# Router logits as plain fp32 matmuls in column groups, with a new order of VectorE's work around the router

## The chip, the cores and the metric

The kernel runs on one NeuronCore of a Trainium2 chip. The metric is the device time of one execution, in microseconds. Each time shown is from the device; the table below gives the median of three runs and, beside it, the one execution that the hardware profiler recorded, from which all rows come.

## What is computed

The input x has 4096 tokens (16 sequences of 256) of 128 channels. It is layer-normed to xn, and two branches work on xn:

```python
# mixer: a linear recurrence over time in each channel
r, alpha, g = sigmoid(lin(x_r, W_r)), sigmoid(lin(x_a, W_a)), sigmoid(lin(x_g, W_g))
k, v, decay = tanh(lin(x_k, W_k)), lin(x_v, W_v), exp(-softplus(lin(x_w, W_w)))
state = state * decay + alpha * k * v          # scan over 256 steps
s = (groupnorm(r * state) * gn_w + gn_b) * g @ W_out.T + b_out
# experts: four rounds, each adds to the current value
for r in range(4):
    logits = cur @ Wg[r] + bg[r]               # 4 experts
    cw = softmax over the two largest, 0 for the others
    hmid = gelu(cur @ W1[e] + b1[e])           # 128 -> 512, every expert
    cur = cur + sum over e of cw[e] * (hmid @ W2[e] + b2[e])
out = x + s * silu(cur)
```

where lin(mix, W) is (xn + (previous xn - xn) * mix) @ W.T. All experts are computed for all tokens; the gates only weigh them.

## The kernel before, in words

**Data and tiles.** Channels lie on the 128 partitions, tokens along the free dimension. `cur` [128, 4096] holds the current value in eight blocks of 512 tokens. Matmuls are in the one-pass type float32r (f32r); to get fp32 products, an operand is split into a high part (f32r) and a low part (the rest), and three matmuls are added: high weight by high data, low weight by high data, high weight by low data (`mm_high` and `mm_low`, L848 to L853).

**Steps.** The expert work is a list of 128 steps (STEPS = 4 rounds x 8 blocks x 4 experts). Step s is turn k = s // 4 (a round and a block) and expert e = s % 4. TensorE's loop (L959) does in step s: `up(s + 1)`, 12 matmuls of 512 columns into four PSUM banks; `down(s)`, 12 matmuls (eight with g_hi, L909 and L910, then four with g_lo, L914) into one of two y banks; then what the tables put there. ScalarE's `hidden(s + 1)` (L374) takes the four banks through gelu in two halves and copies each half to g_hi (L386). VectorE's step s (L766) makes g_lo of step s + 1 in two halves (`g_low_half`, L614, instruction L619), and `combine(s)` (L622, instruction L633) multiplies the y bank by the gates into `tmp`, which POOL's DMA adds to `cur` (L322). down(s) waits for g_hi and g_lo by halves and for combine(s - 2), since there are two y banks (`combined`, L904; it starts at 2 through L757, so down(2) waits for combine(0)).

**Router.** For each turn the logits of four experts are needed. Turns are taken in batches (BATCHES, L36): two of two turns, then seven of four. LOGITS_AT (L53) gives the step of TensorE at which a batch is done: 0, 6, 12, 28, 44, 60, 76, 92 and 108. `logits(n)` (L918) uses f32r operands: `wg_hl` holds Wg's high and low parts side by side (8 columns a round), `wg_pad` is a strip of zeros with these 8 columns in the middle, and a window of 128 columns on it puts the result of turn i on PSUM rows 32 i. Every turn adds its two matmuls (cur_lo, L926; cur_hi, L927) into the same full bank `rb`. `router_scores(n)` (L570) on VectorE transposes the bank, adds high and low columns (L581), adds bg (L582), ranks the four logits and leaves the argument of a tanh; ScalarE's `router_tanh` (L369) takes it; `router_gates(n)` (L602) makes `cw`. SyncE's `spread_gates(k)` (L247) writes cw to DRAM and reads it back on all partitions as `cw_b`, for turn 0 with the first expert's share first (L262). For n of 3 and more VectorE does the scores one step after the logits, behind both halves of g_lo, and the gates two steps after the logits.

**Splitting.** `split_cur(k)` (L545) makes cur_hi and cur_lo of a turn (five buffers); it also copies the round's Wg columns to `wg_pad` (L563).

**Mixer.** Sixteen sequences m, each with stages 0 to 7 at steps 15 + 7 m + stage (`mixers_at`, L58). On VectorE: stages 0 to 2 `mixer_input` (L644; xm_hi L659, xm_lo L661), stage 3 `mixer_scan` (L664; st L673), stage 4 `mixer_norm` (L676, mn L689), stage 6 `mixer_gate`. On TensorE they are projected or transposed at the end of the same step (the norm's result one step later).

**End.** From step 101 on a block b is finished every four steps. `end_scaled(b)` (L705) and `end_product(b)` (L716) stand at the start of VectorE's step 102 + 4 b, TensorE's `turn_product(b)` (L866) transposes the product between up() and down() of step 103 + 4 b, `end_output(b)` (L724) adds x at VectorE's step 103 + 4 b, and SyncE stores it. The last block is done behind the loop.

**Order.** Every engine's order is written out by hand; VectorE's is lines 733 to 844. LATE (L55) holds steps 0 and 8: their combine stands one step later, ahead of the next combine, since their gates come late.

## Time and profile before

| | us |
|---|---|
| median of three runs | 824.88 |
| lowest, highest | 821.72, 825.96 |
| the profiled execution | 823.14 |
| its span, first to last instruction | 821.3 |
| mean granted TensorE clock | 0.993 of full |

How to read the rows below. PE is TensorE's matmul, PEld its weight load, DVE VectorE, ACT ScalarE, POOL GpSimd, SP SyncE. A row of a timeline is: start in us from the span's start, length in us, engine, line of the kernel, operation, output and input by the program's names, shape, count. Brackets hold the idle time before the instruction and what released it. Matmuls overlap in their pipeline and their ends are modelled, so the cost of a matmul is read from start to start, not from its length; a count over 1 merges neighbours of the same line. The granted clock is a share of full speed: 1.00 is the 2.4 GHz level, 0.50 the 1.2 GHz level.

### The profile page before, as it was taken

Reading aid. Unit: us, or ns where it says so; the run is one execution under the profiler, and the core shown is the slowest. Engines: PE = TensorE matmul, PEld = TensorE weight load, DVE = VectorE, ACT = ScalarE, POOL = GpSimd, SP = SyncE. Lnnn points to the kernel's source line nnn. Section 1 sums busy time; section 2 is a strip of 40 time slices with the busy share of each in tenths; the row PEclk is TensorE's granted clock in tenths of the full one; section 3 lists DMA queues with packets and bytes.
Section 4 is the critical chain, followed back from the end, with each engine's and each line's share of the span. In section 5 each row is a group of like instructions: output and inputs, shape, how many; then the busy total and the mean of one; then the engine's idle time right before and its main releaser. Section 6 shows DMA issues by size and latency. Waiting matters only on the chain. (4 is left out here: it accounts for less than half of the span.)

```text
span 821.3 us, 10635 instructions
## 1 busy us (share of the span) xinstructions
PE 803.9 (98%) x3656; PEld 651.3 (79%) x3656; DVE 714.8 (87%) x1339; ACT 652.2 (79%) x911; POOL 115.0 (14%) x135
## 2 busy tenths in 40 slices
PE   8899999999999999999999999999999999899996
PEld 7787788888788887888888887888878888678885
DVE  6978888889997979988898898898989898889897
ACT  7798887887887877888788886888778887678874
POOL 0010211111111111111111101111111111011110
PEclk9999999999999999999999999999999999999998
DMA  9333463342533415423164422644226343174532
GB/s 255 116 78 91 102 162 84 96 97 39 143 59 83 97 33 142 103 49 94 29 152 100 95 39 39 142 103 104 39 54 164 93 116 72 19 180 115 129 65 51
DMA packets 44468, 78.50 MB, mean 96 GB/s; under 512 B 6656, under 2 KB 23552, under 8 KB 40448
## 3 DMA queue, kind: packets, MB, share of 16 engines
q0 software_dynamic: 18144, 33.04, 23.9%
q1 hardware_dynamic: 25136, 44.64, 16.5%
q8 instruction: 29, 0.48, 0.2%
q10 hardware_dynamic: 1136, 0.16, 0.1%
q14 instruction: 23, 0.19, 0.1%
HBM read 40.34 MB, written 2.36 MB: 52 GB/s over the span
## 5 line engine op out<-in xcount | busy, mean ns | idle before, releaser
L382 ACT ACTIVATE g<-h_bank,b_c 128x512 f32<-128x512 f32 x512 | 329.3, 681 | 80.2 <-PE h_bank L853 78.5
L619 DVE TENSOR_TENSOR g_lo<-g,g_hi 128x1024 fp32r<-128x1024 f32 x256 | 307.9, 1221 | 73.6 <-ACT g_hi L386 72.6
L386 ACT ACTIVATE g_hi<-g 128x1024 fp32r<-128x1024 f32 x256 | 271.7, 1062 | 8.1
L322 POOL DMA_DIRECT2D cur<-tmp x126 | 113.9, 904 | 692.1 <-DVE tmp L633 572.4
L849 PE MATMUL h_bank<-cur_hi,w_hi 128*128 128x512 f32 x512 | 206.3, 403 | 1.2 <-ACT g L382 0.7
L909 PE MATMUL y_bank<-g_hi,w_hi 128*128 128x512 f32 x512 | 203.4, 397 | 2.8 <-issue 2.2
L853 PE MATMUL h_bank<-cur_lo,w_hi 128*128 128x512 f32 x512 | 204.1, 399 | 0.0
L850 PE MATMUL h_bank<-cur_hi,w_lo 128*128 128x512 f32 x512 | 203.1, 397 | 0.0
L910 PE MATMUL y_bank<-g_hi,w_lo 128*128 128x512 f32 x512 | 203.0, 397 | 0.0
L914 PE MATMUL y_bank<-g_lo,w_hi 128*128 128x512 f32 x512 | 140.9, 396 | 2.2 <-DVE g_lo L619 2.2
L909 PEld LDWEIGHTS y_bank<-g_hi,w_hi 128*128 128x128 f32 x512 | 96.5, 188 | 26.5 <-issue 2.6
L914 PEld LDWEIGHTS y_bank<-g_lo,w_hi 128*128 128x128 f32 x512 | 96.3, 188 | 26.2 <-DVE g_lo L619 3.1
L853 PEld LDWEIGHTS h_bank<-cur_lo,w_hi 128*128 128x128 f32 x512 | 96.6, 189 | 23.7 <-DVE cur_lo L567 0.4
L910 PEld LDWEIGHTS y_bank<-g_hi,w_lo 128*128 128x128 f32 x512 | 96.6, 189 | 23.4
L849 PEld LDWEIGHTS h_bank<-cur_hi,w_hi 128*128 128x128 f32 x512 | 97.0, 189 | 20.5 <-ACT g L382 1.1
L850 PEld LDWEIGHTS h_bank<-cur_hi,w_lo 128*128 128x128 f32 x512 | 96.7, 189 | 19.2
L633 DVE SCALAR_TENSOR_TENSOR tmp<-y_bank,b_c,cw_b 128x512 f32<-128x512 f32 x128 | 94.9, 743 | 1.4 <-DMA cur<-tmp 1.3
L653 DVE SCALAR_TENSOR_TENSOR xm<-xx,mix,xn_t 128x256 f32<-128x256 f32 x96 | 42.0, 479 | 0.6
L661 DVE TENSOR_TENSOR xm_lo<-xm,xm_hi 128x512 fp32r<-128x512 f32 x48 | 33.2, 693 | 1.6
L853 PE MATMUL p_bank<-xm_lo,pj_hi 128*128 128x256 f32 x96 | 27.6, 288 | 0.9 <-DVE xm_lo L661 0.9
L849 PE MATMUL p_bank<-xm_hi,pj_hi 128*128 128x256 f32 x96 | 27.5, 286 | 0.8 <-DVE xm_hi L659 0.8
L850 PE MATMUL p_bank<-xm_hi,pj_lo 128*128 128x256 f32 x96 | 27.0, 281 | 0.0
(120 smaller groups left out, 516.9 us busy)
## 6 DMA issues: line engine op xcount, KB each, us to landing
cur<-tmp POOLq DMA_DIRECT2D x126, 256.0 KB, 3.4
cw_b<-cw_scratch SPq DMA_DIRECT2D x31, 1024.0 KB, 5.1
cur<-in_x SPq DMA_DIRECT2D x8, 256.0 KB, 5.5
xn_t<-cur SPq DMA_DIRECT2D x8, 256.0 KB, 2.8
xr<-in_x SPq DMA_DIRECT2D x8, 256.0 KB, 3.2
out<-o SPq DMA_DIRECT2D x7, 256.0 KB, 2.4
cw_b<-in_w SPq DMA_DIRECT2D x4, 256.0 KB, 5.2
cw_b<-cw_scratch SPq DMA_DIRECT2D x1, 768.0 KB, 5.2
```

The source lines that it names most:

```text
L322: pool.dma_start(cur[:, block_of(s // E)], tmp[:, s % 2, :], accum_op=ALU.add).then_inc(summed, DMA)
L382: nc.scalar.activation(g[:, gb, ft * BLK:(ft + 1) * BLK], hb[ft][:, :], ACT.Gelu_apprx_tanh, bias=b1_c[:, e * FT + ft:e * FT + ft + 1]).th ...
L386: nc.scalar.activation(g_hi[:, gb, h], g[:, gb, h], ACT.Copy).then_inc(g_hi_done, 1)
L619: nc.vector.tensor_tensor(g_lo[:, gb, h], g[:, gb, h], as_f32(g_hi[:, gb, h]), ALU.subtract).then_inc(g_lo_done, 1)
L633: nc.vector.scalar_tensor_tensor(out=tmp[:, s % 2, :], in0=yb[s % 2][:, :], scalar=b2_c[:, e:e + 1], in1=cw_b[:, q, e * BLK:(e + 1) * BLK] ...
L653: last = nc.vector.scalar_tensor_tensor(out=xm[:, n, :], in0=xx[:, :], scalar=mix[:, k:k + 1], in1=xs[:, 1:LEN + 1], op0=ALU.mult, op1=ALU ...
L849: nc.tensor.matmul(out_ap, w_hi, v_hi, start=True, stop=False)
L850: nc.tensor.matmul(out_ap, w_lo, v_hi, start=False, stop=False)
L853: return nc.tensor.matmul(out_ap, w_hi, v_lo, start=False, stop=True)
L909: nc.tensor.matmul(yb[b][:, :], w2_hi[:, e * FT + ft, :], hi, start=(ft == 0), stop=False)
L910: nc.tensor.matmul(yb[b][:, :], w2_lo[:, e * FT + ft, :], hi, start=False, stop=False)
L914: last = nc.tensor.matmul(yb[b][:, :], w2_hi[:, e * FT + ft, :], g_lo[:, b, ft * BLK:(ft + 1) * BLK], start=False, stop=(ft == FT - 1))
```

## The change

The logits become one plain fp32 matmul for each turn, straight from `cur` with a 32-column weight `wg_p` (4 columns of Wg and 28 of zeros for each round), written to 32 rows of the bank `rb`, that is to column group i of the array. The high and low copies of Wg, the padded strip, its refills in `split_cur` and the add of high and low columns in `router_scores` go. In the order of VectorE: the first gates stand ahead of g_lo(1), behind one low_w2; combine(0) stands ahead of the norm statistics of step 1; combine(8) stands between the halves of g_lo(10); the scores of batches 3 to 8 stand between the halves of g_lo; the norm of a mixer whose stage 4 falls two steps after a logits step stands behind g_lo (this is so once, m = 13 at step 110); the end stage of each block but the last comes one step (the product: from the start of a step to the end of the one before) earlier, with TensorE's transposes of the product.

```diff
@@ -24,7 +24,6 @@
 DMA = 16
 SPLITS = 5
 QUADS = 4
-WG_AT = (QUADS - 1) * RP
 MIX_FROM, MIX_EVERY = 15, 7
 END_FROM = STEPS - E * NB + E
 ADDED_BY_DVE = 2
@@ -59,6 +58,10 @@
     return [(m, s - MIX_FROM - MIX_EVERY * m) for m in range(SEQS) if 0 <= s - MIX_FROM - MIX_EVERY * m < 8]
 
 
+def behind_router(s):
+    return s - 2 in LOGITS_AT.values()
+
+
 def at_step(table, s):
     return [key for key, step in table.items() if step == s]
 
@@ -91,8 +94,8 @@
         pj_hi, pj_lo = sb("pj_hi", [128, 6, D], f32r), sb("pj_lo", [128, 6, D], f32r)
         wo_hi, wo_lo = sb("wo_hi", [128, D], f32r), sb("wo_lo", [128, D], f32r)
         wg_c = sb("wg_c", [128, R, E])
-        wg_hl = sb("wg_hl", [128, R, 2 * E], f32r)
-        wg_pad = sb("wg_pad", [128, WG_AT + 128], f32r)
+
+        wg_p = sb("wg_p", [128, R, RP])
         b1_c = sb("b1_c", [128, E * FT])
         b2_c = sb("b2_c", [128, E])
         bg_b = sb("bg_b", [128, R * E])
@@ -155,7 +158,6 @@
         w2_loaded = [sem(f"w2_loaded{e}") for e in range(E)]
         mixw_loaded, gate_loaded, small_loaded = sem("mixw_loaded"), sem("gate_loaded"), sem("small_loaded")
         made, gates_padded, edge_zeroed = sem("made"), sem("gates_padded"), sem("edge_zeroed")
-        wg_split = sem("wg_split")
         w1_high, w2_high, mixw_high = sem("w1_high"), sem("w2_high"), sem("mixw_high")
         w1_low, w2_low, mixw_low = sem("w1_low"), sem("w2_low"), sem("mixw_low")
         rstd_ready = sem("rstd_ready")
@@ -198,7 +200,7 @@
 
         r_jobs = {}
         for s in range(STEPS):
-            if s > END_FROM and (s - END_FROM) % E == 3:
+            if s > END_FROM and (s - END_FROM) % E == 2:
                 r_jobs["end", (s - END_FROM) // E] = len(r_jobs)
             for n in at_step(LOGITS_AT, s):
                 r_jobs["logits", n] = len(r_jobs)
@@ -559,9 +561,6 @@
                     dve.wait_ge(summed, DMA * E * (k - NB + 1))
                 if k >= SPLITS:
                     dve.wait_ge(up_done, E * FT * (k - SPLITS + 1))
-                if k == 0 or k % NB == QUADS - 1 and k > NB:
-                    nc.vector.tensor_scalar(wg_pad[:, WG_AT:WG_AT + 2 * E], as_f32(wg_hl[:, k // NB, :]), 1.0, None,
-                                            ALU.mult)
                 nc.vector.tensor_scalar(cur_hi[:, q, :], src, 1.0, None, ALU.mult).then_inc(cur_split, 1)
                 dve.wait_ge(cur_split, 2 * k + 1)
                 nc.vector.tensor_tensor(cur_lo[:, q, :], src, as_f32(cur_hi[:, q, :]),
@@ -578,8 +577,7 @@
 
                 nc.vector.transpose(lgt[p, :, :].rearrange("p t c -> p (t c)"), rb[p, :]).then_inc(r_empty, 1)
                 dve.wait_ge(r_empty, job + 1)
-                link(nc.vector.tensor_tensor(l3, lgt[p, :, 0:E], lgt[p, :, E:2 * E], ALU.add))
-                link(nc.vector.tensor_tensor(l3, l3, bg3, ALU.add))
+                link(nc.vector.tensor_tensor(l3, lgt[p, :, 0:E], bg3, ALU.add))
 
                 for e in range(E):
                     if e > 0:
@@ -731,8 +729,8 @@
 
 
             dve.wait_ge(made, 3)
-            for off, width in ((0, WG_AT), (WG_AT + 2 * E, 128 - 2 * E)):
-                nc.vector.tensor_scalar(wg_pad[:, off:off + width], ident[:, 0:width], 0.0, None, ALU.mult)
+            nc.vector.tensor_scalar(wg_p[:, :, E:RP], ident[:, 0:R * (RP - E)].rearrange("p (r c) -> p r c", r=R), 0.0, None,
+                                    ALU.mult)
             norm_stats((0, 1))
             norm_spread((0, 1))
             norm_root((0, 1))
@@ -742,11 +740,7 @@
                                                mean[:, c:c + 1], rstd[:, c:c + 1], ALU.subtract, ALU.mult)
             last.then_inc(xn_first, 1)
             dve.wait_ge(gate_loaded, DMA * GATEW)
-            nc.vector.tensor_scalar(wg_hl[:, :, 0:E], wg_c[:, :, :], 1.0, None, ALU.mult).then_inc(wg_split, 1)
-            dve.wait_ge(wg_split, 1)
-            nc.vector.tensor_tensor(wg_hl[:, :, E:2 * E], wg_c[:, :, :], as_f32(wg_hl[:, :, 0:E]),
-                                    ALU.subtract).then_inc(wg_split, 1)
-            dve.wait_ge(wg_split, 2)
+            nc.vector.tensor_scalar(wg_p[:, :, 0:E], wg_c[:, :, :], 1.0, None, ALU.mult)
             low_w1(0)
             split_cur(0)
             low_w1(1)
@@ -765,7 +759,10 @@
 
             for s in range(STEPS):
 
-                if s == 2:
+                if s == 0:
+                    low_w2(2)
+                    router_gates(0)
+                elif s == 2:
                     norm_root(NORM_GROUPS[1])
                 elif s == 3:
                     norm_stats(NORM_GROUPS[2][0:2])
@@ -786,9 +783,6 @@
                 for k in at_step(SPLIT_AT, s):
                     if NB // 2 <= k < NB:
                         split_cur(k)
-                if s > END_FROM and (s - END_FROM) % E == 2:
-                    end_scaled((s - END_FROM) // E)
-                    end_product((s - END_FROM) // E)
                 for m, stage in mixers_at(s):
                     if stage == 0:
                         mixer_input(m, 0, (P_R, P_W))
@@ -798,7 +792,7 @@
                         mixer_input(m, 2, (P_K, P_V))
                     elif stage == 3:
                         mixer_scan(m)
-                    elif stage == 4:
+                    elif stage == 4 and not behind_router(s):
                         mixer_norm(m)
                     elif stage == 6:
                         mixer_gate(m)
@@ -809,28 +803,34 @@
                 for half in range(2):
                     if s + 1 < STEPS:
                         g_low_half(s + 1, half)
-                    if half == 0 and s == 0:
-                        router_gates(0)
+                    if half == 0:
+                        if s == 9:
+                            combine(8)
+                        for n in at_step(LOGITS_AT, s - 1):
+                            if n >= 3:
+                                router_scores(n)
+                        if s > END_FROM and (s - END_FROM) % E == 1:
+                            end_scaled((s - END_FROM) // E)
 
                 if s == 0:
-                    low_w2(2)
                     low_w2(3)
                 elif s == 1:
+                    combine(0)
                     norm_stats(NORM_GROUPS[1])
                     norm_spread(NORM_GROUPS[1])
                 for k in at_step(SPLIT_AT, s):
                     if k < NB // 2:
                         split_cur(k)
-                if s > END_FROM and (s - END_FROM) % E == 3:
+                if s > END_FROM and (s - END_FROM) % E == 1:
+                    end_product((s - END_FROM) // E)
+                if s > END_FROM and (s - END_FROM) % E == 2:
                     end_output((s - END_FROM) // E)
-                for n in at_step(LOGITS_AT, s - 1):
-                    if n >= 3:
-                        router_scores(n)
+                for m, stage in mixers_at(s):
+                    if stage == 4 and behind_router(s):
+                        mixer_norm(m)
                 for n in at_step(LOGITS_AT, s - 2):
                     if n >= 3:
                         router_gates(n)
-                if s - 1 in LATE:
-                    combine(s - 1)
                 if s not in LATE:
                     combine(s)
             end_scaled(NB - 1)
@@ -919,12 +919,12 @@
 
                 first, turns = BATCHES[n]
                 pe.wait_ge(r_empty, r_jobs["logits", n])
+                if first < NB:
+                    pe.wait_ge(p_empty, first + turns)
                 for i in range(turns):
-                    pe.wait_ge(cur_split, 2 * (first + i + 1))
-                    w = wg_pad[:, WG_AT - RP * i:WG_AT - RP * i + 128]
-                    q = (first + i) % SPLITS
-                    nc.tensor.matmul(rb[:, :], w, cur_lo[:, q, :], start=(i == 0), stop=False)
-                    last = nc.tensor.matmul(rb[:, :], w, cur_hi[:, q, :], start=False, stop=(i == turns - 1))
+                    pe.wait_ge(cur_split, 2 * (first + i) + 1)
+                    last = nc.tensor.matmul(rb[RP * i:RP * (i + 1), :], wg_p[:, first // NB, :], cur[:, block_of(first + i)],
+                                            start=True, stop=True)
                 last.then_inc(r_full, 1)
 
             def project(m, job, kinds):
@@ -961,7 +961,7 @@
                     up(s + 1)
                 if s == 0:
                     logits(0)
-                if s > END_FROM and (s - END_FROM) % E == 3:
+                if s > END_FROM and (s - END_FROM) % E == 2:
                     turn_product((s - END_FROM) // E)
                 down(s)
                 for b in at_step(NORM_SCALE, s):
```

## Rows read from the trace of the kernel before

**Rows 1.** The page, its first part: busy time, share of the span and instructions of each engine.

```profile
PE 803.9 (98%) x3656; PEld 651.3 (79%) x3656; DVE 714.8 (87%) x1339; ACT 652.2 (79%) x911; POOL 115.0 (14%) x135
```

**Rows 2.** TensorE's timeline at the last logits: start us, length, what.

```profile
693.62 0.40 PE L926 MATMUL r_bank<-cur_lo,wg_pad 128*128 128x512 f32 x1
...
695.25 0.40 PE L927 MATMUL r_bank<-cur_hi,wg_pad 128*128 128x512 f32 x1
695.48 0.28 PE L849 MATMUL p_bank<-xm_hi,pj_hi 128*128 128x256 f32 x1
```

**Rows 3.** TensorE's timeline at the first combine; in brackets, idle before.

```profile
31.38 0.40 PE L853 MATMUL h_bank<-cur_lo,w_hi 128*128 128x512 f32 x1
33.93 0.47 PE L909 MATMUL y_bank<-g_hi,w_hi 128*128 128x512 f32 x1 [2.15 <-issue]
34.24 0.60 PE L910 MATMUL y_bank<-g_hi,w_lo 128*128 128x512 f32 x1
...
38.35 0.40 PE L849 MATMUL h_bank<-cur_hi,w_hi 128*128 128x512 f32 x1
```

**Rows 4.** Busy time by windows: stretch, length, TensorE busy, granted clock, DMA share, GB/s.

```profile
34.30:37.60 3.30, 3.30 (x9) 0.50 0.92 306
```

**Rows 5.** VectorE's timeline at the first gates and combines.

```profile
25.25 0.26 DVE L606 SCALAR_TENSOR_TENSOR cw_e<-lg_th,half_sel 64x64 f32<-64x64 f32 x1
...
26.89 1.27 DVE L535 TENSOR_TENSOR w_lo<-xr,w_hi 128x512 fp32r<-128x512 f32 x2
...
30.36 1.63 DVE L504 BATCH_NORM_STATS2 stats<-cur 128x6 f32<-128x128 f32 x8
...
33.08 1.41 DVE L633 SCALAR_TENSOR_TENSOR tmp<-y_bank,b_c,cw_b 128x512 f32<-128x512 f32 x2
```

**Rows 6.** SyncE's timeline: issue of the first gate broadcast.

```profile
27.29 0.35 SPq L262 DMA_DIRECT2D cw_b<-cw_scratch  x1
```

**Rows 7.** DMA issues: count, KB each, median us from issue to landing.

```profile
cw_b<-cw_scratch SPq DMA_DIRECT2D x1, 256.0 KB, 3.7
```

**Rows 8.** TensorE's timeline before down(10).

```profile
84.48 0.50 PE L909 MATMUL y_bank<-g_hi,w_hi 128*128 128x512 f32 x1 [0.61 <-DVE tmp L633]
```

**Rows 9.** TensorE's timeline behind the scores of three batches.

```profile
311.04 0.44 PE L879 MATMUL p_bank<-ident,st 128*128 128x128 f32 x2 [0.92 <-DVE st L673]
...
507.86 0.39 PE L849 MATMUL p_bank<-xm_hi,pj_hi 128*128 128x256 f32 x1 [0.81 <-DVE xm_hi L659]
...
508.58 0.39 PE L853 MATMUL p_bank<-xm_lo,pj_hi 128*128 128x256 f32 x1 [0.23 <-DVE xm_lo L661]
```

**Rows 10.** VectorE's timeline in a router step: the second half of g_lo.

```profile
303.68 1.23 DVE L619 TENSOR_TENSOR g_lo<-g,g_hi 128x1024 fp32r<-128x1024 f32 x1 [1.02 <-ACT g_hi L386]
```

**Rows 11.** TensorE's timeline, down(111) and up(113).

```profile
714.74 0.74 PE L914 MATMUL y_bank<-g_lo,w_hi 128*128 128x512 f32 x2 [1.83 <-DVE g_lo L619]
715.87 0.73 PE L914 MATMUL y_bank<-g_lo,w_hi 128*128 128x512 f32 x2 [0.40 <-DVE g_lo L619]
...
716.89 0.59 PE L850 MATMUL h_bank<-cur_hi,w_lo 128*128 128x512 f32 x1
...
720.26 0.43 PE L849 MATMUL h_bank<-cur_hi,w_hi 128*128 128x512 f32 x1
```

**Rows 12.** VectorE's timeline in step 109.

```profile
699.63 1.23 DVE L619 TENSOR_TENSOR g_lo<-g,g_hi 128x1024 fp32r<-128x1024 f32 x1 [0.26 <-ACT g_hi L386]
...
703.54 0.71 DVE L579 STREAM_TRANSPOSE lgt<-r_bank 128x512 f32<-128x512 f32 x1
...
706.78 0.74 DVE L633 SCALAR_TENSOR_TENSOR tmp<-y_bank,b_c,cw_b 128x512 f32<-128x512 f32 x1
```

**Rows 13.** TensorE's timeline, first matmuls of down(110) and down(118).

```profile
704.85 0.39 PE L909 MATMUL y_bank<-g_hi,w_hi 128*128 128x512 f32 x1
...
758.47 0.40 PE L909 MATMUL y_bank<-g_hi,w_hi 128*128 128x512 f32 x1
```

**Rows 14.** VectorE's timeline in step 117: g_lo(118).

```profile
756.36 2.35 DVE L619 TENSOR_TENSOR g_lo<-g,g_hi 128x1024 fp32r<-128x1024 f32 x2
```

## The prediction

> **What bounds the kernel now.** I read the page first: TensorE is busy for 98% of the span, VectorE 87%, ScalarE 79% [rows 1]. A busy share of pipelined matmuls says little, so the next view is TensorE's timeline, read from start to start. Where nothing is waited for, a matmul of 512 columns starts every 0.233 us: the eight router matmuls of one batch of four take 695.48 - 693.62 = 1.86 us, and what follows starts at once [rows 2]. One step of the loop is 24 such matmuls, 5.6 us, and a stretch without gaps is all streams. So each matmul taken out shortens the kernel by 0.233 us, each one added lengthens it, and any other gain must be a gap in this row. I walked the whole timeline for gaps over 0.25 us. Behind the first 12 us there are few: one of 0.8 us at 17 us, the wait before the last transposes, which the change leaves alone, and those named below. VectorE's work costs nothing by itself; it costs where it is late for one of these gaps.
>
> **Part 1: the logits.** Removed are 32 pairs, 64 matmuls of 512 columns [rows 2]: 64 x 0.233 = 14.9 us, all on the path. Added are 32 matmuls in plain fp32, each with 32 output columns, to four (in the first two batches, two) column groups. The trace has no such matmul. The nearest rows are the kernel's own way to an fp32 product: it splits weights and data into high and low halves, and every pair of halves costs 0.233. All four pairs of halves would be 4 x 0.233 = 0.93 us for one block of tokens.
> - Lower end: the groups run side by side. Every batch takes 0.93: seven batches gain 0.93 each, the two of two blocks gain 0. Sum -6.5.
> - Upper end: one block after another. 3.73 for a batch of four, 1.87 for one of two, in place of 1.87 and 0.93: 7 x 1.87 + 2 x 0.93 = +14.9.
> - Between them: TensorE starts matmuls strictly in order, and the two weight halves of one product are two loads, as they are in this kernel's rows. If a block is two parts of 0.467 us (one per weight half), its second part must follow its first in the same columns, and only the second part overlaps the first of the next block. A batch of four is 5 x 0.467 = 2.33, a batch of two 1.40: 7 x 0.47 + 2 x 0.47 = +4.2.
>
> I take the middle: every row of this trace shows work issued in order, and none shows two matmuls at once; but groups of different columns share nothing that would force the upper end. The Trainium skill ("FP8 and Floating Point Precision", TensorE Precision Notes) says that true FP32 is four passes through the array, which no row here shows. By it the ends stay as they are. Its page "TensorEngine Tiling (Array Packing)" (Key Properties) says that a change of tiling mode drains the engine, with no figure; the nearest switch here is from a transpose back to a matmul, 0.08 us, and I leave it in the range.
>
> **Part 2: the first gates and combine.** down(2) waits for the first combine. up(3) issues its last matmul at 31.38, so down(2) could start at 31.61; it starts at 33.93 [rows 3], 2.32 us late. Behind this gap the granted clock is 0.50, the 1.2 GHz level [rows 4]: 11 matmuls from 34.24 to 38.35 take 4.11 where 2.57 is normal, another 1.54. Together 3.86.
> Why it is late: VectorE runs norm statistics and spread from 30.36 to 33.08, and only then the two combines [rows 5]. The change puts the combine at 30.36. Is its gate there? The first gate broadcast is issued at 27.29 [rows 6] and such a transfer lands 3.7 us later [rows 7], at 31.0. Gates now start at 25.25, behind half of g_lo; ahead of it, and behind one 0.60 us low_w2 that moves with them [rows 5], they start at 24.72, and the score chain is 0.25 us shorter (one add less, below). So the broadcast lands near 30.2, when VectorE gets to the combine; it ends near 31.0, before 31.6. low_w2(2) merely changes places, and g_lo(1) ends when it did; the statistics, 0.7 us later, feed an xn block that is turned only two steps later. Gain 3.86. If the broadcast came 1 us later, 0.3 us of the gap would stay.
>
> **Part 3: combine(8)** stands today behind both halves of g_lo(10), and down(10) idles 0.61 before it; ends are modelled 0.16 late, so from start to start it is 0.78 [rows 8]. Between the halves VectorE has idle time; gain 0.78.
>
> **Part 4: the scores between the halves.** Today a router step of VectorE is g_lo half 0, idle until ScalarE has half 1, half 1, the scores, the combine, and then the mixer's instructions, which come late. With 0.16 added as in part 3, the mixed-state transpose is 1.08 late, an xm_hi 0.97, and an xm_lo 0.39, which two more batches repeat [rows 9]. Sum 1.08 + 0.97 + 3 x 0.39 = 3.2. The idle time before half 1 is 1.02 in these batches [rows 10]; with the scores in it, and 0.25 shorter, VectorE is 1.27 earlier at all of these: gain 3.2. What queues behind the scores is half 1 of g_lo. Today it ends 1.2 to 2.3 us before the step's down(); behind the scores it ends between 0.4 us before and 1.7 after the start of down(), and is read 2.3 after that start. By my walk over the seven batches 0.6 to 2.8 us are left, so no new wait.
> The add that falls away (0.26 in nine batches), the wg_pad fills and the split of Wg are VectorE's alone; at the start the low-half split stands before a wait for the transposes, and I give it 0.
>
> **Part 5: norm behind g_lo, and the end stage a step earlier.** The largest gap of the second half: two pairs of g_lo matmuls at 714.74 and 715.87 start 1.99 and 0.66 late, and then the clock is at the lower level again: 8 matmuls from 716.89 to 720.26 take 3.37 for 1.87 [rows 11]. Sum 4.15. mixer_norm stands in front of g_lo(111) there, behind the scores; it is the one norm that the new test moves. Gain 4.15.
> The price: the products z are now turned one step earlier, between up() and down(). The turn waits for end_product, and that for half 1 of g_lo. At step 110 both the scores (703.54 to 706.78, so 3.24, now 3.0) and end_scaled (0.60) stand between the halves: 699.63 + 1.14 + 3.0 + 0.60 + 1.14 + 0.69 = 706.2 [rows 12]; TensorE is at the turn at 704.85 [rows 13], so it waits 1.4. At step 118 g_lo runs from 756.36 without idle time [rows 14]: 756.36 + 2.27 + 0.60 + 0.69 = 759.9 against 758.47 [rows 13], 1.5. At 114 it is 0.3; at the other four the product is ready 0.7 to 1.1 early. Cost 3.2. The mixed-norm transposes of step 111 want mn at about 715; moved, it is done near 714.7. SyncE's stores and reloads follow the earlier turns and wait for nothing new.
>
> **Sum.** -3.86 - 0.78 - 3.2 - 4.15 + 3.2 = -8.8 for the order of the work, +4.2 for the logits: -4.6. The profiled execution took 823.14 (span 821.3), so 818.5; the median of the runs shown is 824.88, 1.7 above it, and so the forecast for the median is 820.3. A measurement of this kernel can tell about 0.5% (4.1 us) from no change; the forecast is 0.56% faster.
>
> **The rivals.**
> - **Groups side by side.** -8.8 - 6.5, less about 1.1, since a shorter logits stretch brings TensorE 0.9 us sooner to mixer inputs that VectorE has just in time: -14.2, 810.7. For it: different columns need nothing of each other. Against: no row shows two matmuls at once. The skill's "TensorE: Matmul & The Clock Gate" (Part 3) says this would happen: three column groups of N=512 measured 2.38 times as fast. No row here tests it.
> - **Slower: the logits one block after another.** One mechanism, at the end of nine steps of TensorE's queue: +14.9 - 8.8 = +6.1, 831.0. It decides from the point where a batch of four costs 1.1 us more than today (2.98): there the nine batches eat the whole 8.8. For it: full serial order in every row.
> - **The first combine does not come earlier**, since the gate's way through DRAM (the write, then the broadcast of 3.7) sets it, or the clock falls again behind one of the two new 1.5 us waits: 3 to 4 us of gain go, 824. Against it: the gaps behind which the clock fell were 2.3 and 2.65 long, and behind 1.08 at 310 us it did not fall.
>
> **How the numbers follow.** In-order parts (820.3): 0.40. Side by side (810.7): 0.25. One after another (831.0): 0.25. Order of work fails (824): 0.10. The range goes from the side-by-side case less 2 us (no new waits at steps 110 and 118 would give 3.2) to the serial case itself: 808.5 to 831. Leaving out its tails, it should hold 8 in 10. The forecast case alone spans 817 to 823. Faster by over 0.5% (below 820.8): all of the second case and somewhat over half of the first, 0.50. Slower (above 829.0): most of the third, 0.22. Within: 0.28.
>
> **What would show it.** Right: a batch of four logits takes 2.2 to 2.5 us from its first start to the next line; no gap at 31.6 and full clock behind it; no gap before down(10); none at 309, 507 and 712; new waits of about 1.5 us before the turns of steps 110 and 118. Side by side would show four logits starts within some 0.2 us; the serial case would show 0.93 between them. The prediction is wrong at its root if TensorE gets new gaps over 0.3 us in front of g_lo matmuls at steps 30 to 110, that is, if half 1 behind the scores comes too late.

## The result, and the profile after

| us | before | after |
|---|---|---|
| median | 824.76 (4 runs beside it) | 809.26 (4 runs, 809.04 to 810.82) |
| ratio, 95% interval | | 0.9827 [0.981, 0.9845] |
| the profiled execution, its span | 823.14, 821.3 | 809.22, 807.4 |

The kernel became 15.5 us faster by the medians; the ratio on record says 1.7% [1.6, 1.9]. The forecast was 4.6 us, a median of 820.3, so the measured one lies 11.0 below it. The two traces differ by 13.9 in span; the rest is spread between executions, and the account below is of these two traces.

The page's first part, which answers to [rows 1]:

```profile
PE 794.1 (98%) x3656; PEld 638.7 (79%) x3656; DVE 711.8 (88%) x1324; ACT 651.7 (81%) x911; POOL 114.4 (14%) x135
```

The shares hardly move. TensorE has as many matmul records as before, 3656: 64 f32r matmuls went, and each of the 32 fp32 matmuls has two records. The costliest groups of TensorE, by shape, show them (count | busy us, mean ns | idle before):

```profile
L926 PE MATMUL r_bank<-cur,wg_p 128*32 128x512 f32 x64 | 9.6, 605 | 0.0
```

A record is 605 ns long, yet all 64 fill 9.6 us, so they overlap. TensorE's timeline at the last logits, against [rows 2]:

```profile
681.09 1.06 PE L926 MATMUL r_bank<-cur,wg_p 128*32 128x512 f32 x8
682.08 0.39 PE L849 MATMUL p_bank<-xm_hi,pj_hi 128*128 128x256 f32 x1
682.31 0.28 PE L850 MATMUL p_bank<-xm_hi,pj_lo 128*128 128x256 f32 x1
682.42 0.28 PE L853 MATMUL p_bank<-xm_lo,pj_hi 128*128 128x256 f32 x1
```

The row of eight merges its records. Taken singly in the trace, the first records of the four blocks start at 681.089 to 681.109 and the second ones at 681.541 to 681.561: **all four column groups at once**. The batch takes 0.99 from its start to the next line, where it took 1.86. Around it 0.2 is given back: the matmul ahead of the batch takes 0.09 more from start to start, and the first one behind it 0.22 where 0.12 is normal. Net, each of seven batches saves 0.66 to 0.71; the two of two blocks cost 0.24 each.

The waits of TensorE summed over the span, all that the view has (us in total, times, longest):

```profile
PE r_bank L871 <- DVE th L719: 3.8, 3, 1.3
PE h_bank L988 <- DVE th L719: 3.2, 1, 3.2
PE r_bank L952 <- POOL ident L313: 1.8, 1, 1.8
PE h_bank L849 <- ACT g L384: 0.7, 1, 0.7
PE h_bank L849 <- DVE cur_hi L564: 0.4, 1, 0.4
PE p_bank L863 <- ACT o L360: 0.4, 1, 0.4
```

Everything of [rows 3, 8, 9, 11] is gone. The one new entry is the first: the turns of the product, TensorE's timeline in steps 110, 114 and 118:

```profile
692.91 0.65 PE L871 MATMUL r_bank<-ident,th 128*128 128x128 f32 x4 [1.24 <-DVE th L719]
...
718.55 0.66 PE L871 MATMUL r_bank<-ident,th 128*128 128x128 f32 x4 [1.25 <-DVE th L719]
...
744.62 0.66 PE L871 MATMUL r_bank<-ident,th 128*128 128x128 f32 x4 [1.32 <-DVE th L719]
```

From start to start these are 1.41, 1.43 and 1.50. Why the middle one is there stands in ScalarE's timeline:

```profile
713.75 0.64 ACT L422 ACTIVATE th<-cur 128x512 f32<-128x512 f32 x1 [2.38 <-DMA cur<-tmp]
714.30 1.24 ACT L384 ACTIVATE g<-h_bank,b_c 128x512 f32<-128x512 f32 x2
715.57 1.06 ACT L388 ACTIVATE g_hi<-g 128x1024 fp32r<-128x1024 f32 x1
```

The tanh of the end stage stands between the halves of `hidden` and waits 2.38 us for POOL's add into `cur`; behind it come g and g_hi, then VectorE's g_lo (at 716.66, after 1.92 idle on that g_hi), then the product (717.81), then the turn.

Walking the first `up` matmul of every step in both traces gives the ledger, in us of TensorE's time:

| | forecast | found |
|---|---|---|
| first combine and clock | -3.86 | -3.93 |
| combine(8) | -0.78 | -0.88 |
| scores between the halves, four batches | -3.2 | -4.0 |
| steps 111 and 112 | -4.15 | -4.24 |
| new waits before the turns | +3.2 | +4.34 |
| logits | +4.2 | -4.3 |
| a 0.38 gap at step 114 gone, the start, small rest | 0 | -0.8 |
| sum | -4.6 | -13.8 |

### The profile page after: what moved, and what is told of

Read it like the earlier page. It is cut to its first block, busy times and chain, and to the rows that moved or that the text cites. A ratio compares the mean times of both kernels' runs of the same rounds, so it can differ in the third digit from the quotient of the medians.

```text
span 807.4 us, 10619 instructions
## 1 busy us (share of the span) xinstructions
PE 794.1 (98%) x3656; PEld 638.7 (79%) x3656; DVE 711.8 (88%) x1324; ACT 651.7 (81%) x911; POOL 114.4 (14%) x135
## 4 chain that ended last, share of the span: by engine, by line
PE 91%; DVE 3%; ACT 2%; DMA 2%; issue 1%; SPq 0%; DVEq 0%; ACTq 0%; POOLq 0%
PE y_bank L914 14%; PE y_bank L910 14%; PE y_bank L909 14%; PE h_bank L853 14%; PE h_bank L849 14%; PE h_bank L850 14%; PE p_bank L849 2%; PE p_bank L853 2%; PE p_bank L850 2%; DMA cur<-tmp 1%; PE r_bank L926 1%; ACT g L384 1%; PE p_bank L879 1%; DMA cw_b<-in_w 1%; ACT g_hi L388 1%
```

## The experiments

The theory for the gap between forecast and result: the column groups run side by side, and the order of the work is worth what the ledger says. Rivals: fp32 itself is cheap, without groups; the program's order of the matmuls decides how they overlap; single moves do nothing. "x1" to "x12" number the twelve kernels; x6 stands behind x9, with x10 to x12, which build on it. Before was run beside each: its median was 823.33 beside x1, x2, x3 and x6, 824.8 beside x9 to x11 and 824.34 beside x12, and its one execution beside x4, x5, x7 and x8 took 824.87. After was not run again, so against its 809.26 a difference in time of about 1 us says nothing by itself; the walk over the steps is given where it matters.

**x1: the new order with the old logits.** Edit: the f32r pairs, `wg_pad` and the add of high and low columns are back.

```diff
-                    last = nc.tensor.matmul(rb[RP * i:RP * (i + 1), :], wg_p[:, first // NB, :], cur[:, block_of(first + i)],
-                                            start=True, stop=True)
+                    nc.tensor.matmul(rb[:, :], w, cur_lo[:, q, :], start=(i == 0), stop=False)
+                    last = nc.tensor.matmul(rb[:, :], w, cur_hi[:, q, :], start=False, stop=(i == turns - 1))
```

> The new order of work with the old f32r logits. Theory (the logits now run side by side: in the changed kernel a batch of four takes 0.99 us between its first start and the next line, with the switches about 0.67 less than before, seven times, and the two batches of two cost about 0.2 more each): this kernel gives up 7 x 0.68 - 2 x 0.2 = 4.4 us, about 813.7, and keeps the new waits before the turns at steps 110, 114 and 118. Rival (the logits are a minor part and the time came from gaps in the order that I had missed): within 2 us of the changed kernel, 811 or less.

Measured: 815.41 (before 823.33), ratio 0.9902 [0.9886, 0.9917]: the order alone is worth 1.0%. Against after, each batch of four costs 0.66 to 0.71 more and the turns wait 1.65, 1.90 and 1.49. It took 1.7 more than expected: by the walk, about 1.0 is an early dip of the clock in the profiled execution (see x9), and waits at steps 78, 110 and 114 cost about 1.0 more than in after.

**x2: the new logits with the old order.** Edit: all moves in VectorE's, TensorE's and SyncE's order undone.

> The fp32 logits in the old order of work. If the two parts of the change simply add: 824.8 - 4.4 = 820.4. Theory: they do not quite add, since behind a shorter logits stretch TensorE arrives 0.7 us sooner at mixer inputs for which VectorE is already late, so the gaps near 309 and 507 us and the one near 712 grow by up to 0.7 each while the small ones at 210 and 608 grow too: about 822 to 823.

Measured: 816.65, ratio 0.9921 [0.9897, 0.9945]: 6.5 us gained, more than either theory had. The batches save 0.67 to 0.71 as in after. With x1's 1.0% its 0.8% adds up to the 1.7% of the whole. What I missed: the gaps of before don't grow by the shorter logits. The five steps with the gaps near 84, 211, 311, 508 and 608 us get shorter by 0.24 to 0.27 each, the time of the add that fell away from the scores. TensorE's timeline in x2:

```profile
34.18 0.48 PE L899 MATMUL y_bank<-g_hi,w_hi 128*128 128x512 f32 x1 [1.83 <-issue]
34.49 0.40 PE L900 MATMUL y_bank<-g_hi,w_lo 128*128 128x512 f32 x1
34.73 0.40 PE L899 MATMUL y_bank<-g_hi,w_hi 128*128 128x512 f32 x1
...
307.01 0.33 PE L869 MATMUL p_bank<-ident,st 128*128 128x128 f32 x1 [0.68 <-DVE st L667]
```

0.68 at 307.01 answers to the 0.92 of [rows 9]. So the shorter logits don't bring TensorE nearer to VectorE. My reading, not tested by itself, is that VectorE follows ScalarE, and ScalarE follows TensorE's banks. And behind the gap of 2.00 at 34.18 the clock did not fall in this execution. Its window (stretch, length, then busy time of PE, PEld, DVE, ACT, POOL; granted clock, DMA share, GB/s) answers to [rows 4]:

```profile
34.30:37.60 3.30, 3.30 (x15) 2.65 (x16) 2.96 (x13) 0.72 (x1) 1.01 (x1) 1.00 1.01 310
```

That is 1.5 of the 7.5 between the spans of the two traces. It need not be so in every execution: the four took 815.24 and 815.58 at a mean clock of 0.996, and 817.72 and 817.84 at 0.992 and 0.993. Only the one of 815.58 has a trace, so where the clock fell in the two longer ones is not shown.

**x3: fp32 without column groups.** Edit: `wg_p` in a padded strip of 128 columns, all turns added into the full bank.

```diff
-                    last = nc.tensor.matmul(rb[RP * i:RP * (i + 1), :], wg_p[:, first // NB, :], cur[:, block_of(first + i)],
-                                            start=True, stop=True)
+                    last = nc.tensor.matmul(rb[:, :], wg_p[:, WG_AT - RP * i:WG_AT - RP * i + 128],
+                                            cur[:, block_of(first + i)], start=(i == 0), stop=(i == turns - 1))
```

> The changed kernel with the same plain fp32 logits, but through the padded 128-column strip, so that all turns of a batch use all columns and add up in the bank. Theory (the column groups make the batch short, not fp32): 0.93 us per block one after another, 3.7 for a batch of four, so 7 x 2.6 + 2 x 0.8 = 20 us more than the changed kernel, about 829. Rival (plain fp32 is cheap in itself): a batch of four near 1.9 us, about 815.

Measured: 824.13 in one execution (before 823.33). TensorE's timeline at the last logits:

```profile
694.20 3.60 PE L928 MATMUL r_bank<-cur,wg_p 128*128 128x512 f32 x8
697.23 0.68 PE L851 MATMUL p_bank<-xm_hi,pj_hi 128*128 128x256 f32 x1
697.75 0.28 PE L852 MATMUL p_bank<-xm_hi,pj_lo 128*128 128x256 f32 x1
```

3.03 to the next line and 0.52 for a matmul that normally takes 0.12: 3.43 for four blocks, eight parts of 0.43. This is my serial case, at 0.86 a block and not 0.93, and with nothing lost before or inside the batch. **The side by side is worth 2.23 to 2.25 a batch of four, and 15 us by the times** (the nine batches add up to some 17; other steps of x3 ran up to 0.04 shorter each, about 2 in all, for which I have no cause). Without it the change would have gained nothing. That the parts add up to 3.7 one-pass matmuls agrees with the Trainium skill ("FP8 and Floating Point Precision", TensorE Precision Notes), which gives four passes.

**x4, x5: each logits matmul issued twice**, in a row (blocks 0,0,1,1,...) and in turn (0,1,2,3,0,1,2,3). The product is written twice with the same values.

```diff
+                    for _ in range(2):   # x4, inside the loop over i
...
-                for i in range(turns):
+                for i in [j for _ in range(2) for j in range(turns)]:   # x5
```

> Each fp32 logits matmul is issued twice, the second right behind the first to the same columns (0, 0, 1, 1, 2, 2, 3, 3); the output is the same. Theory A (a matmul that waits for its columns does not hold up later ones of other columns, or all are taken up at once): twice the work of each column group, side by side, a batch of four takes 1.9 to 2.0 us in place of 0.99. Theory B (matmuls are handed to the array strictly in order, and the parts of the four blocks ran together in the changed kernel only because the queue held them in the order 0 1 2 3, 0 1 2 3): each block's second product holds up the next block, and the batch takes about 0.9 x 5 = 4.3 us or, if the four parts of neighbouring blocks are mixed, between 2.5 and 4.3.

> Each fp32 logits matmul is issued twice, but in turn (0, 1, 2, 3, 0, 1, 2, 3); the output is the same. Both theories: 1.9 to 2.0 us for a batch of four, 7 x 0.95 + 2 x 0.95 = 8.5 us more than the changed kernel, about 818. If the run with the repeats in a row takes the same, theory A holds; if it takes clearly more, theory B.

Measured: 816.96 and 816.94, one execution each, 1 under the expectation, since a batch costs 0.88 or 0.86 more and not 0.95. The timelines at the last logits, of x4:

```profile
687.80 1.94 PE L927 MATMUL r_bank<-cur,wg_p 128*32 128x512 f32 x16
689.67 0.38 PE L849 MATMUL p_bank<-xm_hi,pj_hi 128*128 128x256 f32 x1
```

and of x5:

```profile
687.75 1.92 PE L926 MATMUL r_bank<-cur,wg_p 128*32 128x512 f32 x16
689.61 0.38 PE L849 MATMUL p_bank<-xm_hi,pj_hi 128*128 128x256 f32 x1
```

From the first start to the next line it is 1.87 and 1.86 (1.874 and 1.854 unrounded): the order in the program makes next to no difference. In x4 the single records start in fours, at 687.80, 688.25, 688.68 and 689.11, though two neighbours of the program share a group. Within a four the starts are 0.013 apart in x4 and 0.007 in x5: in x4 the program has two products between the first ones of two groups, in x5 one. So the matmuls of one group queue for it while those of other groups pass. The second issue adds 0.88, and the first batch took 0.99: 0.88 is one fp32 product (0.86 in x3), the other 0.11 is paid once. With the 0.09 and 0.11 around it a batch in column groups pays 0.3 beyond its work, which is why batches of two lose 0.24 (0.88 + 0.3 against 0.94).

**x7: the first gates and combine undone.**

```diff
-                if s == 0:
-                    low_w2(2)
-                    router_gates(0)
-                elif s == 2:
+                if s == 2:
...
-                    combine(0)
                     norm_stats(NORM_GROUPS[1])
                     norm_spread(NORM_GROUPS[1])
+                    combine(0)
```

> The changed kernel with the first gates back behind half 0 of g_lo(1) and the first combine back behind the norm statistics. Theory (down(2) waits for that combine): a gap of about 2.0 us before down(2), since the score chain is still 0.25 shorter; the run with only the new logits showed that behind a gap of 2.00 the clock stays at the 2.4 GHz level, so 2.0 us in all, about 811.3; if the clock falls, 1.5 more, 812.8. Rival (the first gates' way through DRAM sets it): no change, 809.3.

Measured: 813.48 in one execution, 4.2 above after; by the walk over the steps 3.6 of it lies at step 2, and 0.8 in the first 20 us, a dip of the clock that x9 below shows too. TensorE's timeline:

```profile
34.91 0.48 PE L909 MATMUL y_bank<-g_hi,w_hi 128*128 128x512 f32 x1 [1.83 <-issue]
35.23 0.40 PE L910 MATMUL y_bank<-g_hi,w_lo 128*128 128x512 f32 x1
35.46 0.48 PE L909 MATMUL y_bank<-g_hi,w_hi 128*128 128x512 f32 x1
35.74 0.63 PE L910 MATMUL y_bank<-g_hi,w_lo 128*128 128x512 f32 x1
36.17 0.63 PE L909 MATMUL y_bank<-g_hi,w_hi 128*128 128x512 f32 x1
```

The gap returns (1.99), and from 35.74 the spacing is 0.43. The window, read as in x2, has the granted clock at 0.50, the 1.2 GHz level:

```profile
35.70:39.00 3.30, 3.30 (x9) 2.57 (x8) 2.99 (x12) 0.05 (x1) 0.71 (x1) 0.50 0.94 306
```

The same wait of 1.83 was followed by full clock in x2.

**x8: the scores behind both halves of g_lo again.**

```diff
-                        for n in at_step(LOGITS_AT, s - 1):
-                            if n >= 3:
-                                router_scores(n)
...
+                for n in at_step(LOGITS_AT, s - 1):
+                    if n >= 3:
+                        router_scores(n)
```

> The changed kernel with the scores of batches 3 to 8 back behind both halves of g_lo. Theory: VectorE loses the idle time of 1.0 us between the halves in four of the six batches, so the gaps come back, each 0.25 smaller than in the kernel before: 0.85 at the scan near 303, 0.73 and 0.38 near 498, 0.38 near 205 and 596; at step 110 the wait before the transposes of the product gets shorter, because the product no longer stands behind the scores: 1.4 less. Net 2.7 - 1.4 = +1.3, about 810.6. Rival (the gaps were made by something else): 808.

Measured: 814.87 in one execution, 4.3 us over what I expected. The gaps of [rows 9] return, 0.38, 0.84, 0.72 with 0.37, and 0.39; the wait at step 110 goes, as the theory had it. But a step later, TensorE's timeline:

```profile
706.20 0.69 PE L879 MATMUL p_bank<-ident,mn 128*128 128x128 f32 x2 [2.25 <-DVE mn L687]
706.54 0.78 PE L849 MATMUL h_bank<-cur_hi,w_hi 128*128 128x512 f32 x1
707.12 0.63 PE L850 MATMUL h_bank<-cur_hi,w_lo 128*128 128x512 f32 x1
```

The norm, now behind g_lo and the scores, is 2.41 late, and the clock falls behind it (granted 0.50 from 706.20 to 709.50). So the new place of the norm is no gain on its own: with the scores behind, it turns the gap of [rows 11] into one of its own size.

**x9: the norm of m = 13 in front of g_lo again.**

```diff
 def behind_router(s):
-    return s - 2 in LOGITS_AT.values()
+    return False
```

> The changed kernel with the norm of m = 13 back in front of g_lo(111). My prediction gave the whole 4.15 us of the gap at 712 to this move. Theory after the last runs (with the scores between the halves, VectorE reaches step 110 1.3 us sooner, and TensorE now waits 1.4 before the product's transposes, so g_lo(111) is ready in time even behind the norm): within 0.5 us of the changed kernel, 809.3. Rival (the move itself closed the gap): two gaps before g_lo matmuls near 700 come back and the clock falls behind them, 811 to 813.

Measured: 810.39 in one execution, no gap comes back. It is 1.2 longer in span, and 1.0 of that lies in the first 20 us. The window of after, read as in x2:

```profile
11.00:14.00 3.00, 2.56 (x14) 1.85 (x15) 2.50 (x5) 3.00 (x8) 0.00 (x0) 1.00 1.22 290
```

and of x9:

```profile
11.00:14.00 3.00, 2.48 (x11) 1.92 (x12) 2.17 (x5) 3.00 (x8) 0.00 (x0) 0.67 1.22 290
```

A dip of the clock there, long before anything that the edit touches. It is in 5 of the 14 profiled executions of this study (x1, x6, x7, x9 and x12) and costs 0.8 to 1.2. What decides it is open. The rest is 0.2 at step 114.

**x6: the turn of the product behind down()**, where TensorE comes 12 matmuls, 2.8 us, later.

```diff
+                down(s)
                 if s > END_FROM and (s - END_FROM) % E == 2:
                     turn_product((s - END_FROM) // E)
-                down(s)
```

> The changed kernel with TensorE's transposes of the product moved from in front of down() to behind it, in the same step. Theory (the three waits of 1.41, 1.43 and 1.50 us before these transposes are on the path and nothing hides behind them): 4.3 us less, about 805.0, and no wait in their place, because the product is ready 2.8 us before down() ends. Rival (the waits give VectorE the slack that the following steps live on): the wait turns up again before a g_lo matmul or a mixer input of steps 111 to 120, and the time stays within 1.5 us of 809.3.

Measured: 807.0 (806.59 to 808.1), ratio 0.9803 [0.9786, 0.9819], between the two expectations and 2.3 below after, with no run in common. The three waits, 4.3 us, go; 1.9 come back, from start to start, as waits for mn (0.72) and for xm_hi and xm_lo (0.78, 0.39) in steps 111 and 114, TensorE's timeline:

```profile
702.17 0.44 PE L879 MATMUL p_bank<-ident,mn 128*128 128x128 f32 x2 [0.56 <-DVE mn L687]
...
721.92 0.39 PE L849 MATMUL p_bank<-xm_hi,pj_hi 128*128 128x256 f32 x1 [0.55 <-DVE xm_hi L657]
...
722.65 0.39 PE L853 MATMUL p_bank<-xm_lo,pj_hi 128*128 128x256 f32 x1 [0.23 <-DVE xm_lo L659]
```

**x10: the end stage undone**, all else as in after.

> The changed kernel with the end stage of each block at its old steps (product at the start of step 102 + 4 b, transposes one step later). Theory (the end stage a step earlier costs three waits and brings nothing): the three waits go, 4.3 us, and about 1 us comes back as small waits of TensorE for VectorE between 697 and 725, as in the run with the transposes behind down(): 806. Rival (the earlier end stage unloads step 110, so that without it the gap near 712 comes back): 809 or more.

Measured: 808.64 (808.12 to 809.62), 0.981 [0.9792, 0.9827], 2.6 above the expectation. The three waits go, and one large one comes in their place, TensorE's timeline:

```profile
721.20 0.38 PE L848 MATMUL p_bank<-xm_hi,pj_hi 128*128 128x256 f32 x1 [1.64 <-DVE xm_hi L657]
```

From start to start it is 1.81; 0.39 for the xm_lo behind it and 0.32 for an mn in step 111 come with it. The span is 806.3 against 807.4. So the earlier end stage, whose waits cost 4.3, saves some 3 elsewhere in steps 110 to 115; it is a small loss, within the spread of the runs. No gap near 712 comes back, so it was not the end stage that closed it.

**x11: x6, and the product and the output behind the mixer's work** in VectorE's order.

```diff
+                if s > END_FROM and (s - END_FROM) % E == 2:   # ahead of g_lo, behind the mixers
+                    end_product((s - END_FROM) // E)
```

> The transposes of the product behind down(), as in the run before, and on VectorE the product behind the mixer's input of the same step (in front of g_lo) and the output behind the norm. That run gave back 1.9 us in three small waits: 0.72 for mn and 0.78 and 0.39 for an xm_hi and xm_lo. Theory (each of them is made by a 0.6 us instruction of the end stage that stands in front): about 1.6 of the 1.9 go, 805.3. Rival (VectorE is full in these steps and the waits only move): 807.

Measured: 808.11 (807.73 to 809.22), 0.9805 [0.9788, 0.9822], 2.8 above the expectation and 1.1 above x6: the waits only move, as the rival had it. One wait of 1.87 is left before the turn of block 3, and ScalarE's timeline has the same row as after, longer:

```profile
714.04 0.64 ACT L422 ACTIVATE th<-cur 128x512 f32<-128x512 f32 x1 [3.69 <-DMA cur<-tmp]
```

**x12: x11, and the tanh behind `hidden`.**

```diff
-                    if s > END_FROM and (s - END_FROM) % E == 1:   # between the halves
-                        end_tanh((s - END_FROM) // E)
...
+                if s > END_FROM and (s - END_FROM) % E == 1:
+                    end_tanh((s - END_FROM) // E)
```

> The version before (product behind the mixer's instructions, transposes behind down) with one thing more: on ScalarE the tanh of the end stage stands behind both halves of hidden instead of between them. In that version one wait of 1.87 us is left, before the transposes of block 3 (TensorE at 721.47), and one of 0.38 before an xm_lo; ScalarE's tanh of that block stood between the halves and waited 3.69 us for POOL's add. Theory: the half of hidden queued behind that waiting tanh makes g_hi, g_lo and so the product late; with the tanh behind hidden the half no longer waits, and the 1.87 goes: about 1.9 us less, 806.2. Rival: the add itself (POOL, DMA) sets when the tanh and the product of block 3 can be made, wherever the tanh stands: the 1.87 stays or grows, 808 or a little more.

Measured: 806.97 (805.77 to 806.99, 5 runs), 0.9785 [0.9766, 0.9803], 2.3 below after, with no run in common. By the medians it is no faster than x6 (807.0), which has neither x11's move nor this one. ScalarE's timeline:

```profile
711.45 1.25 ACT L384 ACTIVATE g<-h_bank,b_c 128x512 f32<-128x512 f32 x2
712.73 1.06 ACT L388 ACTIVATE g_hi<-g 128x1024 fp32r<-128x1024 f32 x1
715.39 0.64 ACT L422 ACTIVATE th<-cur 128x512 f32<-128x512 f32 x1 [1.59 <-DMA cur<-tmp]
```

The tanh still waits for the add, 1.59 now, but g_hi is in front of it, at 712.73 and not at 715.57. The turn of block 3 follows its down() without a wait:

```profile
719.91 1.10 PE L914 MATMUL y_bank<-g_lo,w_hi 128*128 128x512 f32 x4
720.85 0.60 PE L871 MATMUL r_bank<-ident,th 128*128 128x128 f32 x4
```

Behind the first 20 us and ahead of the last turn only one gap over 0.3 is left, 0.38 at 714.66. This profiled execution has the early dip of the clock, so its span of 805.2 is about 1.1 above what it would be without; the same holds for x6 and its 806.3.

## Why the prediction was wrong

**Part 1, the logits: the step that failed** is "TensorE starts matmuls strictly in order", so that only one part of a block overlaps the next block. I took the middle, +4.2, because "every row of this trace shows work issued in order, and none shows two matmuls at once". The rows could not show it: before the change no two matmuls used different column groups. Measured: -4.3, of which seven batches give -4.8 and two of two give back 0.5. That term is 8.5 of the 9.2 us between forecast and ledger. Two of its pieces held: a product is two parts (0.43, the first of a batch in groups 0.45; forecast 0.467), and serial order costs 3.43 a batch (x3; forecast 3.73). What fell is that a part must wait for its place in the program's order: the four first parts start within 0.02, the four second ones 0.45 later, and repeats in a row take the same as repeats in turn (x4, x5). The rival "groups side by side" is what happened. Its -6.5 missed the 0.3 of switching per batch, a cost that I had left to the range beside a row of 0.08 for another kind of switch; and its deduction of 1.1 for a TensorE that comes too soon was wrong (x2: the gaps shrink). That its sum, -14.2, comes near the ledger's -13.8 is partly luck: the logits gave 2.2 less than it said, and 1.1 of deduction and 0.8 of small rest made up for it. The Trainium skill's rule in "TensorE: Matmul & The Clock Gate" (Part 3) speaks of three groups at 2.38 times the rate; four groups here give 3.43 to 0.99, 3.5 times, or 3.43 to 1.19, 2.9 times, with the way in and out counted. So the trace agrees that groups run at once, and the rule should have had more weight than rows that could not speak to the question. Its page "TensorEngine Tiling (Array Packing)" (Key Properties) says that a change of tiling mode drains the engine. That fits the 0.3 us, which x3, without groups, does not pay; that it is this drain is not shown.

**Part 2, first combine: right** at -3.93. Undoing it costs 3.6 (x7). Nearly half of it rests on a clock that falls or doesn't behind the same wait of 1.83 (x7, x2), so the safe part is the gap itself, 2.0 to 2.3. Before itself varies: its executions took from 821.6 at a mean clock of 0.997 (beside x1) to 826.27 at 0.992 (beside x9), after's from 809.04 to 810.82. So the 1.5 of clock here, and that in part 5, is a reading of the profiled execution, which had both falls, and may not be in each.

**Part 3, combine(8): right** in the ledger, -0.88; it was not tried alone.

**Part 4, the scores: right in mechanism, somewhat small in size**, -4.0 for -3.2. Undoing them brings each gap back where the trace of before had it (x8). The 0.8 is 0.37 at each of the two batches where I had counted only an xm_lo, 0.38: there xm_hi is also 0.17 late, below my limit of 0.25, and the first matmul behind each of the two waits takes 0.10 to 0.11 longer from start to start.

**Part 5, the norm: right sum, wrong cause, so luck.** The 4.15 came (4.24), but not from the moved norm: with it back in front no gap returns (x9), with the end stage back none does (x10), and with the norm moved but the scores behind, a gap of 2.41 opens (x8). The scores between the halves carry it. In x9 TensorE also waits 1.39 before the turn of step 110, which gives VectorE time; whether the norm's place matters without that wait was not tried. **The price** was 4.34 for 3.2: steps 110 and 118 as worked out (1.4 and 1.5), step 114 1.43 for 0.3. I walked VectorE's queue there and not ScalarE's, where a tanh that waits for a DMA holds half of `hidden`; x12 moves that tanh, in the order of x11, and the wait goes. That the waits are a loss the forecast said, and x6 shows it: with TensorE's turn behind down() 2.3 us come back. But 4.34 is not the net price of the earlier end stage: undoing it whole gives back only 1.1 in span (x10). That the order came out at -8.7 for -8.8 is luck too: 0.8 more from the scores and 0.3 from the other gains met 1.1 more of price.

**The range** of 808.5 to 831 held 809.26, near its lower end, in the rival case that I had given 0.25.

What stays open: why POOL's add into `cur` lands when it does at step 114 (no run touches the adds), what decides whether the clock falls behind a wait of 1.8, and whether column groups would do as much for the f32r pairs: no run puts them into groups.

## What to carry to other kernels

A trace whose matmuls all use the whole array says nothing about column groups; there, weigh a rule that measured them above an order seen in other rows, and give the forecast to the side with a measurement. Price a batch in column groups as its longest group plus about 0.3 us, so pack enough matmuls into one. Before an instruction that waits for a DMA is put between two halves of a hot stage, walk each engine's queue behind it, not only that of the engine being tuned; and credit a closed gap to a move only after that move alone has been undone. Nor is a wait's length what its removal gives: of 4.3 taken away in x6, 1.9 came back elsewhere.

## What was unexpected of the hardware

- fp32 matmuls of 128 by 32 by 512 in four column groups run fully side by side, and matmuls of one group don't block those issued behind them for other groups: 0.99 for four blocks, +0.88 or 0.86 for four more, in a row or in turn, against 3.43 with 128 columns each.
- A batch in column groups costs 0.3 us beyond its work.
- After a wait of 1.83 before the same matmul the clock fell for 3.4 us in x7 and not at all in x2. It did not fall behind gaps of 1.81, 1.87 and 1.90 (x10, x11, x1) and did behind 2.32 and 2.41 (before, x8), and behind two gaps in a row, 1.99 with 0.66 in before ([rows 11]) and 1.73 with 0.56 in x2. It also fell near 12 us in 5 of 14 executions, which cost 0.8 to 1.2 us, whatever the edit: more than some of the differences looked for here.
